# Second layer: third pair's projection and square moved ahead of pair 0's scores, and a new order of powers, masks, gathers and folds on GpSimd

## The chip, the cores and the metric

The kernel runs on one core of one Trainium2 chip. The metric is the device time of one execution in microseconds (us), lower is better. A core has a matrix engine (TensorE, PE in the rows), VectorE (DVE), ScalarE (ACT), GpSimd (POOL) and SyncE (SP), each with its own instruction queue that runs in order; they wait for each other through semaphores. What this kernel can tell from no change is about 0.2%, some 2.5 us.

## The reference

Two transformer-like layers over 8 batch items of 512 tokens with 128 features. In each layer an attention and a feed-forward branch work on the same normalised input, and both are added to it. Layer 1 has a banded 16-head attention and a top-1 mixture of eight experts. Layer 2, which the change touches, is this (the reference, cut):

```python
# layer 2, attention: 16 query heads of 64, one shared key/value head
xn = layernorm(x, g1)
q = xn @ Wq.T ; kv = xn @ Wkv.T            # k, v = 64 features each
q, k = l2norm(q) * 4, l2norm(k) * 4        # each head's vector divided by its length
sim = einsum('bhid,bjd->bhij', q, k)       # causal mask
out = einsum('bhij,bjd->bhid', softmax(sim), v)
attn = layernorm(out.reshape(b, n, 1024) @ Wout.T, g2)
# layer 2, feed-forward: weights are integers times 1/127
ffn = (silu(x @ wg.T) * (x @ wu.T)) @ wd.T
x = x + attn + ffn
```

## The kernel before, in words

Layer 1's attention takes the first part of the program, its experts the next, and layer 2 the last: from 619 us of the span on. Layer 2 runs once per batch item, seven times in a hardware loop and a last time (item 8) written out without the preparation of a next item. One trip is about 77 us.

The 16 heads go in 8 pairs (NP = 8), and `attend` on each engine has a loop `for n in range(NP)`, round n for pair n. Every engine's order of work is written out by hand, and a ring per PSUM bank or group of banks (Q, O, L, S, M, W, Z; `fillable`, `filled`, `emptied`) gives the semaphore values to wait for. In one round:

- TensorE: `scores(n)` (keys by queries, in three thirds), `project_q(n + 2)`, which makes the queries of the pair after next, `turn_q(n + 1)` (a transpose), for the first rounds a third of the feed-forward (`gate_up`), then `values1(n - 1)`. `sums1(0)` comes in round 5 and `sums1(1)` in round 6: they add up the exponentials of pairs 0 and 1, and of 2 and 3, for the softmax's denominators.
- ScalarE: three `exp_of(n, third)`, `squares(n + 2)` of the projected queries, `q_turned(n + 1)`, `gate_up(n + 1)`.
- VectorE: `q_sums` adds up the squares, `q_low(n + 1)`, `values_out(n - 1)`, then `q_unit(n + 2)`: it takes the length from GpSimd (L1958, L1960: scale and reciprocal) and multiplies the projected queries (L2011). That frees the projection's only PSUM bank (ring Q has one), so `project_q(n + 3)` can't start before it.
- GpSimd: `q_length` (L1272: the square root of the sums, as a power), then the causal masks of pair n (L1313, four selects in three groups, each group behind the exponentials of its third). Between them it prepares the next item: `fetch_slots` and `fetch` gather the experts' rows (L1231, two in round 1 and two in round 2), `both_roots` in round 4. And `fold(n)` (L1293) for pairs 0 to 3: a DMA from GpSimd's queue that adds block 1 of a pair's exponentials to block 0, so that `sums1` has less to read. In before `fold(n - 2)` is the first thing of rounds 2 to 5.

The name `arena` in rows is one big SBUF buffer, `late` its continuation for two pairs' exponentials, `ring_d` the projection's bank, `q_len`, `q_sum`, `q_rn` the lengths, their squares and reciprocals, `q_nat_sb` and `o_n` the two buffers of normalised queries.

Of the kernel before, what the change touches and what calls it, by code (L numbers as in the profile page):

```python
# [100 lines left out]
             sums=6, lens=6, q_lo=8, h1=3, masked=24, pv=4, added4=6, g_free=2, inverted=1, fin=1, stored=16,  # L101
             folded=16 * N_FOLD)

# [150 lines left out]
def two_layers(nc, x, wq, bq, wk, bk, wv, bv, wo, bo, w_router, w1, b1, w2, b2,  # L254
# [4 lines left out]
    with ExitStack() as ctx:  # L259
# [232 lines left out]
        def _(pe):  # L492
# [296 lines left out]
            def attend(b, last):  # L789
# [80 lines left out]
                def sums1(m):  # L870
# [3 lines left out]
                    if m < N_FOLD // 2:  # L874
                        pe.wait_ge(s["folded"].sem, s["folded"].at(b, 32 * (m + 1)))
                    if m == 2:
# [9 lines left out]
                pe.wait_ge(SR["r_free"].sem, SR["R"].emptied(b, "k.T"))  # L886
                gate_up(0)
                pe.wait_ge(SR["r_free"].sem, SR["R"].emptied(b, "q.T"))
                for n in range(NP):
                    scores(n)  # L890
                    if n + 2 < NP:
                        project_q(n + 2)
# [167 lines left out]
        def _(pool):  # L1060
# [219 lines left out]
            def attend(b, last):  # L1280
# [6 lines left out]
                def fold(n):  # L1287

                    pool.wait_ge(s["o_full"].sem, s["O"].filled(b, ("o", n)))
                    if n:  # L1290
                        pool.wait_ge(s["folded"].sem, s["folded"].at(b, 16 * n))
                    apart(pool)
                    pool.dma_start(probs_of(n, 0)[:, :, P:T], probs_of(n, 1),  # L1293
                                   accum_op=ALU.add).then_inc(s["folded"].sem, s["folded"].add(16))

                s["folded"].restart()
                for n in range(NP):
                    if 0 <= n - 2 < N_FOLD:
                        fold(n - 2)
                    if n + 2 < NP:  # L1300
# [15 lines left out]
                    if not last and n == 0:  # L1316
                        fetch_slots(b + 1)
                    if not last and n in (1, 2):
                        fetch(b + 1, (2 * n - 2, 2 * n - 1))
                    if not last and n == 4:  # L1320
# [17 lines left out]
        def _(act):  # L1338
# [156 lines left out]
            def attend(b, last):  # L1495
# [40 lines left out]

                gate_up(0)
                for n in range(NP):
                    for third in (0, 1, 2):
                        exp_of(n, third)  # L1540
                    if n + 2 < NP:
                        squares(n + 2)
                    if n + 1 < NP:
                        q_turned(n + 1)
                    if n + 1 < HC:
                        gate_up(n + 1)
# [658 lines left out]
```

## Time and profile before

| what | value |
|---|---|
| median of 3 runs | 1240.59 us (1240.56 to 1241.66) |
| the profiled execution's own time | 1239.02 us |
| its span, first to last instruction | 1237.2 us |
| TensorE busy, share of the span | 93% |
| VectorE, ScalarE, GpSimd busy | 74%, 54%, 40% |
| granted TensorE clock, mean | 0.98 |
| one trip of layer 2's loop | 77.0 us |

TensorE's busy share is an average over both layers. In one trip of layer 2 it is busy 72.8 of 77.0 us, and the rest is a handful of waits that return in each trip at the same place. A timeline's row gives a run of like instructions: start, length, engine, line, what it writes and reads, how many, and in brackets the idle time of the engine before it with the engine and line that ended it.

### The profile page before, as it was taken

The page shows a single profiled execution, that of the slowest core. Times are in us where ns is not written, and L with a number is a line of the kernel's source. Part 1 is how long each engine was busy: PE and PEld are TensorE (multiplying, and loading weights), DVE is VectorE, ACT ScalarE, POOL GpSimd, SP SyncE. Part 2 cuts the span into 40 slices and gives each one's busy share as a digit, 9 for nine tenths or more (in the row PEclk, how much of TensorE's full clock was granted, in tenths as well). Part 3 has the DMA queues.
Part 4 walks back from the last instruction along what each step waited for, and adds up shares of the span by engine and source line. Part 5 has one row for each costly group of instructions (what it writes and reads, how often), then busy time and mean ns, then how long its engine had stood idle before and what let it go on. Part 6 is the DMA issues. An engine that isn't in the chain of part 4 may idle for free.

```text
span 1237.2 us, 26393 instructions
## 1 busy us (share of the span) xinstructions
PE 1145.6 (93%) x8475; PEld 782.4 (63%) x8475; DVE 921.7 (74%) x2473; ACT 672.3 (54%) x1290; POOL 490.6 (40%) x691
## 2 busy tenths in 40 slices
PE   5999999999999998899399999999999999999996
PEld 3656666666666554799265857657576575765764
DVE  7888888888888897455456868668686686866755
ACT  2767676666676755355173552735527355273550
POOL 5122212121222311554364481744817448274450
PEclk8999999999999998899799999999999999999999
DMA  3311212020101000122011030210302103021020
GB/s 89 101 44 48 56 28 57 26 60 26 33 18 27 18 18 1 44 64 55 15 35 27 9 59 0 42 25 8 59 0 42 25 8 59 0 49 19 15 46 10
DMA packets 43718, 42.31 MB, mean 34 GB/s; under 512 B 7040, under 2 KB 36224, under 8 KB 43648
## 3 DMA queue, kind: packets, MB, share of 16 engines
q0 software_dynamic: 11008, 17.31, 8.0%
q1 hardware_dynamic: 32640, 24.15, 7.3%
q8 instruction: 34, 0.56, 0.2%
q14 instruction: 36, 0.29, 0.1%
HBM read 13.72 MB, written 6.75 MB: 17 GB/s over the span
## 4 chain that ended last, share of the span: by engine, by line
issue 19%; PE 11%; POOL 9%; DVE 7%; DMA 3%; ACT 1%; POOLq 0%; DVEq 0%; ACTq 0%
PE pair L496 4%; POOL q_len L1272 3%; DMA arena<-arena 3%; PE gather L496 2%; PE ring_d L496 2%; POOL arena L1231 2%; POOL arena L1313 2%; PE ring_a L496 1%; PE pair L500 1%; DVE q_len L1958 1%; DVE stats L1574 1%; POOL arena L1293 1%; DVE arena L2106 1%; DVE q_rn L1960 1%; ACT arena L1515 1%
## 5 line engine op out<-in xcount | busy, mean ns | idle before, releaser
L1378 ACT ACTIVATE arena<-ring_a 128x384 f32<-128x384 f32 (+1 forms) x512 | 253.6, 550 | 147.1 <-PE ring_a L496 146.9
L1126 POOL TENSOR_SCALAR_AFFINE_SELECT arena<-arena 128x512 f32<-128x512 f32 x128 | 82.4, 643 | 366.6 <-ACT arena L1378 366.4
L496 PE MATMUL ring_a<-q_max,rows 128*128 128x384 f32 (+1 forms) x512 | 197.2, 388 | 2.2 <-DVE q_max L1684 1.8
L1670 DVE CUSTOM_DVE_ANT_0 arena<-pair,arena 128x384 bf16<-128x384 f32 (+1 forms) x269 | 161.3, 614 | 23.6 <-PE pair L496 19.1
L1272 POOL TENSOR_TENSOR q_len<-q_sum,exponents 128x8 f32<-128x8 f32 x64 | 113.6, 1775 | 85.1 <-DVE q_sum L2000 85.1
L1535 ACT ACTIVATE arena<-ring_a 128x1024 f32<-128x1024 f32 x96 | 99.1, 1032 | 75.9 <-PE ring_a L496 75.7
L496 PE MATMUL ring_a<-q_parts,k_rows 64*128 64x384 f32 (+2 forms) x1152 | 128.3, 344 | 3.4 <-ACT q_parts L1523 2.4
L496 PE MATMUL ring_a<-arena,v_aug 128*32 128x384 f32 (+1 forms) x1024 | 123.5, 553 | 1.7 <-POOL arena L1126 0.6
L496 PE MATMUL pair<-arena,v_aug 128*64 128x512 f32 (+3 forms) x768 | 114.0, 439 | 3.4 <-ACT arena L1535 3.0
L496 PE MATMUL pair<-rows,q_rows 128*128 128x384 f32 (+1 forms) x269 | 110.0, 411 | 3.3 <-DMA rows<-k_rows 2.5
L496 PEld LDWEIGHTS ring_a<-q_max,rows 128*128 128x128 f32 x512 | 96.8, 191 | 21.4 <-ACT arena L1378 5.3
L496 PEld LDWEIGHTS ring_a<-q_parts,k_rows 64*128 64x128 f32 x1152 | 90.0, 187 | 23.7 <-issue 12.6
L1313 POOL TENSOR_SCALAR_AFFINE_SELECT arena<-arena 128x256 f32<-128x256 f32 x192 | 80.9, 531 | 45.5 <-ACT arena L1535 43.9
L496 PEld LDWEIGHTS pair<-arena,v_aug 128*64 128x64 f32 x768 | 51.1, 136 | 71.9 <-issue 58.7
L1670 DVE CUSTOM_DVE_ANT_0 arena<-gather,arena 128x512 bf16<-128x512 f32 (+1 forms) x124 | 78.2, 630 | 17.6 <-PE gather L496 11.4
L496 PEld LDWEIGHTS pair<-rows,q_rows 128*128 128x128 f32 x269 | 51.2, 191 | 57.4 <-DVE mx L1670 34.9
L2056 DVE COPY arena<-pair 128x512 f32<-128x512 f32 x64 | 44.2, 691 | 52.3 <-PE pair L496 51.8
L1670 DVE CUSTOM_DVE_ANT_0 arena<-ring_d,arena 128x384 bf16<-128x384 f32 (+1 forms) x119 | 73.2, 615 | 9.8 <-PE ring_d L496 6.5
L2000 DVE TENSOR_REDUCE q_sum<-arena 128x8 f32<-128x512 f32 x64 | 43.8, 684 | 44.6 <-ACT arena L1507 44.6
L496 PE MATMUL ring_d<-wq_sb,o_raw 128*128 128x128 f32 x384 | 55.6, 288 | 18.0 <-DVE o_n L2011 9.9
L496 PEld LDWEIGHTS ring_d<-wq_sb,o_raw 128*128 128x128 f32 x384 | 46.5, 191 | 37.5 <-DVE q_nat_sb L2011 18.3
L1440 ACT ACTIVATE arena<-ring_a,arena 128x128 f32<-128x128 f32 x156 | 43.6, 377 | 47.3 <-PE ring_a L496 46.9
(275 smaller groups left out, 2380.9 us busy)
## 6 DMA issues: line engine op xcount, KB each, us to landing
arena<-arena POOLq DMA_DIRECT2D x32, 384.0 KB, 4.6
rows<-k_rows SPq DMA_DIRECT2D x128, 64.0 KB, 2.0
arena<-in_w SPq DMA_DIRECT2D x16, 256.0 KB, 2.8
slots_y<-arena SPq DMA_DIRECT2D x39, 64.0 KB
x_all<-in_x SPq DMA_DIRECT2D x8, 256.0 KB, 3.8
tokens_x<-xn SPq DMA_DIRECT2D x8, 256.0 KB, 2.7
out<-o_t SPq DMA_DIRECT2D x8, 256.0 KB, 2.3
arena<-tokens_x,tokens_now POOLq DMA_INDIRECT x40
```

The lines of the kernel that those rows point to most:

```text
L496: return pe.matmul(out, lhs, rhs, start=start, stop=stop, skip_group_check=True)
L500: return [pe.transpose(slot[:, i * P:(i + 1) * P], tile_of(i), ident[:]) for i in range(n)][-1]
L1126: pool.affine_select(out=v, in_=v, compare_op=ALU.is_ge, fill=0.0, base=0, pattern=[[0, HG], [1 if late else -1, P]], channel_multiplier=- ...
L1231: pool.indirect_dma_start(y_back[:, i, :], None, slots_y[0:(TT + NE - 1) * P], bass.IndirectOffsetOnAxis(ap=slots_now[:, i:i + 1], axis=0) ...
L1272: pool.tensor_tensor(q_len[:, half], q_sum[:, half], exponents[:, 2 * NT:4 * NT], ALU.pow).then_inc(s["lens"].sem, s["lens"].add(1))
L1313: ins = pool.affine_select(out=v, in_=v, compare_op=ALU.is_ge, fill=0.0, base=0, pattern=[[0, 2], [1, P]], channel_multiplier=-1)
L1378: act.activation(probs[:, t % NT, h, 0:many], A.slot(("cols", c))[:, 0:many], ACT.Exp).then_inc(A.free.sem, A.free.add(1))
L1440: ins = act.activation(hidden[:, u % 2, c], hidden_bank(u, c), ACT.Relu, bias=staged[:, u, AT_B1 + c:AT_B1 + c + 1])
L1535: act.activation(dst, src, ACT.Exp).then_inc(ring.free.sem, ring.free.add(1))
L1670: dve.tensor_tensor_reduce(dump[:, h % 2, 0:many], M.slot(("max", n))[:, 0:many], masks[:, m, at:at + many], 1.0, LOWEST, ALU.add, ALU.max ...
L2000: dve.reduce_sum(q_sum[:, half_of(s, k)], q_sq, AX.X).then_inc(s["sums"].sem, s["sums"].add(1))
L2056: dve.tensor_copy(o1[:, n, :], ring.slot(("o", n))[:]).then_inc(ring.free.sem, ring.free.add(1))
```

## The change

Three things move; no arithmetic is added or taken away.

1. TensorE's `project_q(2)` and ScalarE's `squares(2)` stood in round 0 behind pair 0's scores and exponentials. They now stand behind `gate_up(0)`, ahead of round 0.
2. In each round GpSimd does the power first, then the masks, then gathers, then folds. Folds 0 and 1 come at the end of rounds 2 and 3, folds 2 and 3 at the end of round 4; before, one stood at the head of each of rounds 2 to 5. The gathers are one, two, one in rounds 0, 1, 2 and no longer two, two in rounds 1 and 2.
3. A fold no longer waits until the fold before it has landed: folds 0 and 1 count on one semaphore, 2 and 3 on another, and `sums1(0)` and `sums1(1)` wait for 32 on theirs.

```diff
-             folded=16 * N_FOLD)
+             folded0=32, folded1=32)
...
                     if m < N_FOLD // 2:
-                        pe.wait_ge(s["folded"].sem, s["folded"].at(b, 32 * (m + 1)))
+                        pe.wait_ge(s[f"folded{m}"].sem, s[f"folded{m}"].at(b, 32))
...
                 gate_up(0)
+                project_q(2)
                 pe.wait_ge(SR["r_free"].sem, SR["R"].emptied(b, "q.T"))
                 for n in range(NP):
                     scores(n)
-                    if n + 2 < NP:
+                    if 0 < n < NP - 2:
                         project_q(n + 2)
...
                 def fold(n):
                     pool.wait_ge(s["o_full"].sem, s["O"].filled(b, ("o", n)))
-                    if n:
-                        pool.wait_ge(s["folded"].sem, s["folded"].at(b, 16 * n))
+                    folded = s[f"folded{n // 2}"]
...
                 for n in range(NP):
-                    if 0 <= n - 2 < N_FOLD:
-                        fold(n - 2)
                     if n + 2 < NP:
                         q_length(s, n + 1, b)
...
                     if not last and n == 0:
                         fetch_slots(b + 1)
-                    if not last and n in (1, 2):
-                        fetch(b + 1, (2 * n - 2, 2 * n - 1))
+                    if not last and n < 3:
+                        fetch(b + 1, ((0,), (1, 2), (3,))[n])
+                    for of in {2: (0,), 3: (1,), 4: (2, 3)}.get(n, ()):
+                        fold(of)
...
                 gate_up(0)
+                squares(2)
                 for n in range(NP):
                     for third in (0, 1, 2):
                         exp_of(n, third)
-                    if n + 2 < NP:
+                    if 0 < n < NP - 2:
                         squares(n + 2)
```

TensorE's queue at the head of a trip, before and after (L798 and L802 are waits of the projection and of `gate_up`, L840 to L852 those of the scores):

```order
 L802 ISA
 L496 MATMUL ring_a<-q_rows,w_gu 128x512 x4
-L888 REGISTER_ALU
+L798 ISA
+L496 MATMUL ring_d<-wq_sb,o_raw 128x128 x4
+L889 REGISTER_ALU
 L840 REGISTER_ALU
 L841 ISA
```

The projection of pair 2 (ring_d) now stands between the feed-forward's first third and the wait ahead of pair 0's scores.

GpSimd's queue before, from the masks of round 2 to the power of round 3 (DMA arena<-slots_y is a gather, DMA arena<-arena a fold, TENSOR_TENSOR q_len the power):

```order
L1313 AFFINE_SELECT arena<-arena 128x2x128
L1231 DMA arena<-slots_y,slots_now 128x128 x2
L1289 REGISTER_ALU
L1291 ISA
L1293 DMA arena<-arena 128x2x384
L1270 REGISTER_ALU
L1272 TENSOR_TENSOR q_len<-q_sum,exponents 128x8
```

Two gathers, the wait for the last fold (L1291) and fold 1 stand ahead of the power. The same place of the changed kernel, whose lines have moved by one:

```order
L1312 AFFINE_SELECT arena<-arena 128x2x128
L1232 DMA arena<-slots_y,slots_now 128x128
L1290 ISA
L1293 DMA arena<-arena 128x2x384
L1271 REGISTER_ALU
L1273 TENSOR_TENSOR q_len<-q_sum,exponents 128x8
```

One gather and fold 0 stand there now. And the end of round 4 of the changed kernel, up to the power of round 5:

```order
L1312 AFFINE_SELECT late<-late 128x2x128
L1290 REGISTER_ALU
L1293 DMA arena<-arena 128x2x384
L1290 REGISTER_ALU
L1293 DMA arena<-arena 128x2x384
L1099 TENSOR_SCALAR veps<-mv 128x4
L1100 TENSOR_SCALAR veps<-mv 128x4
L1101 ISA
L1102 TENSOR_TENSOR rstd<-veps,exponents 128x8
L1271 REGISTER_ALU
L1273 TENSOR_TENSOR q_len<-q_sum,exponents 128x8
```

Folds 2 and 3 have moved ahead of `both_roots` (veps, rstd); before, fold 2 stood ahead of round 4's power and fold 3 between `both_roots` and round 5's power.

## Rows read from the trace of the kernel before

**Rows 1.** The page: busy time of each engine, and the projections' group.
```profile
PE 1145.6 (93%) x8475; PEld 782.4 (63%) x8475; DVE 921.7 (74%) x2473; ACT 672.3 (54%) x1290; POOL 490.6 (40%) x691
...
L496 PE MATMUL ring_d<-wq_sb,o_raw 128*128 128x128 f32 x384 | 55.6, 288 | 18.0 <-DVE o_n L2011 9.9
```

**Rows 2.** Busy time in windows, the third trip: length, then each engine's busy time.
```profile
773.90:850.90 77.00, 72.77 (x632) 51.36 (x632) 56.19 (x115) 38.35 (x60) 40.50 (x55) 1.00 0.15 27
```

**Rows 3.** Chain that ended last, third trip: start, length, what.
```profile
799.00 2.31 POOL q_len L1272
...
812.76 4.43 DMA arena<-arena
```

**Rows 4.** Timeline of TensorE: third trip, then seventh, then item 8.
```profile
773.91 1.11 PE L496 MATMUL ring_a<-q_parts,k_rows 64*128 64x384 f32 x12 [0.16 <-DVEq L2032]
...
776.34 1.16 PE L496 MATMUL ring_d<-wq_sb,o_raw 128*128 128x128 f32 x8
...
779.24 1.23 PE L496 MATMUL ring_a<-q_parts,k_rows 64*128 64x384 f32 x12 [0.28 <-ACT q_parts L1523]
...
782.15 1.16 PE L496 MATMUL ring_d<-wq_sb,o_raw 128*128 128x128 f32 x8 [0.54 <-DVE q_nat_sb L2011]
...
795.40 1.16 PE L496 MATMUL ring_d<-wq_sb,o_raw 128*128 128x128 f32 x8 [0.34 <-DVE q_nat_sb L2011]
...
802.92 1.16 PE L496 MATMUL ring_d<-wq_sb,o_raw 128*128 128x128 f32 x8 [1.50 <-DVE o_n L2011]
...
817.23 1.72 PE L496 MATMUL gather<-arena,pick_sum 128*32 128x512 f32 x24 [0.50 <-DMA arena<-arena]
...
1103.93 1.16 PE L496 MATMUL ring_d<-wq_sb,o_raw 128*128 128x128 f32 x8 [1.08 <-DVE q_nat_sb L2011]
...
1110.84 1.16 PE L496 MATMUL ring_d<-wq_sb,o_raw 128*128 128x128 f32 x8 [0.89 <-DVE o_n L2011]
...
1179.87 1.16 PE L496 MATMUL ring_d<-wq_sb,o_raw 128*128 128x128 f32 x8
```

**Rows 5.** Timeline of GpSimd, third trip.
```profile
795.53 1.39 POOL L1231 DMA_INDIRECT arena<-slots_y,slots_now  x1 [0.18 <-issue]
...
798.16 1.42 POOL L1293 DMA_DIRECT2D arena<-arena  x1
799.00 2.29 POOL L1272 TENSOR_TENSOR q_len<-q_sum,exponents 128x8 f32<-128x8 f32 x1
...
803.41 1.25 POOL L1293 DMA_DIRECT2D arena<-arena  x1 [0.65 <-DMA arena<-arena]
...
807.17 1.49 POOL L1313 TENSOR_SCALAR_AFFINE_SELECT late<-late 128x256 f32<-128x256 f32 x4
810.53 0.24 POOL L1098 TENSOR_SCALAR veps<-mv 128x4 f32<-128x4 f32 x1 [1.88 <-DVE mv L1583]
...
813.60 2.12 POOL L1272 TENSOR_TENSOR q_len<-q_sum,exponents 128x8 f32<-128x8 f32 x1
```

**Rows 6.** Timeline of VectorE, third trip, and one row of the seventh.
```profile
797.23 0.69 DVE L2000 TENSOR_REDUCE q_sum<-arena 128x8 f32<-128x512 f32 x1 [0.55 <-ACT arena L1507]
...
799.35 0.69 DVE L2056 COPY arena<-pair 128x512 f32<-128x512 f32 x1 [0.43 <-PE pair L496]
801.33 0.49 DVE L1958 TENSOR_SCALAR q_len<-q_len 128x8 f32<-128x8 f32 x1 [1.28 <-POOL q_len L1272]
...
1101.39 1.44 DVE L1958 TENSOR_SCALAR q_len<-q_len 128x8 f32<-128x8 f32 x1
```

**Rows 7.** Timeline of ScalarE, rounds 0 and 1 of the third trip.
```profile
775.27 1.03 ACT L1535 ACTIVATE arena<-ring_a 128x1024 f32<-128x1024 f32 x1
...
777.61 0.60 ACT L1507 ACTIVATE arena<-ring_d 128x512 f32<-128x512 f32 x1
...
783.35 0.60 ACT L1507 ACTIVATE arena<-ring_d 128x512 f32<-128x512 f32 x1 [0.41 <-PE ring_d L496]
```

**Rows 8.** The folds' line: who waited for it (us, times).
```profile
  PE gather L496: 4.0, 7
```

More of the change, by code:

```diff
@@ L1289, in fold @@
                     pool.wait_ge(s["o_full"].sem, s["O"].filled(b, ("o", n)))
-                    if n:
-                        pool.wait_ge(s["folded"].sem, s["folded"].at(b, 16 * n))
+                    folded = s[f"folded{n // 2}"]
                     apart(pool)
                     pool.dma_start(probs_of(n, 0)[:, :, P:T], probs_of(n, 1),
-                                   accum_op=ALU.add).then_inc(s["folded"].sem, s["folded"].add(16))
-                s["folded"].restart()
+                                   accum_op=ALU.add).then_inc(folded.sem, folded.add(16))
+                for name in ("folded0", "folded1"):
+                    s[name].restart()
                 for n in range(NP):
-                    if 0 <= n - 2 < N_FOLD:
-                        fold(n - 2)
                     if n + 2 < NP:
```

## The prediction, made before the changed kernel ran

> **What bounds the kernel now.** I read the page first: TensorE is busy 93% of the span and no other engine is near [rows 1]. That is an average over two layers, so I cut layer 2 into trips with the view by windows: a trip is 77.0 us with TensorE busy 72.77 [rows 2], so at most 4.2 us of a trip can be won by a new order. Next the timeline of TensorE, for the idle times in brackets [rows 4]. In the third trip they are 0.16 us ahead of pair 0's scores, 0.28 ahead of pair 1's, 0.54 ahead of pair 3's projection, 0.34 ahead of pair 5's, 1.50 ahead of pair 6's and 0.50 ahead of the second sums. The 1.50 returns in each of the first six trips, and the seventh has 1.08 and 0.89 in place of 0.34 and 1.50; the page's group agrees, 9.9 us of waits for the buffer o_n being 6 x 1.50 + 0.89 [rows 1]. Item 8 has no wait at these places: there GpSimd has no gathers, and pair 5's projection follows its predecessor at once [rows 4]. Then the chain of waits, to see what the two largest hang on: GpSimd's power in round 3, and a fold's DMA ahead of the second sums [rows 3].
>
> **The change part by part.**
>
> *GpSimd's power in round 3.* Its input, the sum of squares, starts at 797.23 and is there at 797.92 [rows 6]. But GpSimd is still at its second gather, then issues fold 1 from 798.16 for 1.42 us, to 799.58, and only then is the power worked off: it ends at 799.00 + 2.29 = 801.29, so it takes 1.71 from the end of the fold [rows 5]. VectorE, idle 1.28, starts on the length at 801.33 [rows 6], and TensorE starts pair 6's projection at 802.92, 1.59 later, having been ready at 802.92 - 1.50 = 801.42 [rows 4].
> In the changed order round 2 ends with one gather and fold 0. The gather starts at 795.53 as before and takes 1.39 [rows 5]; the fold follows at about 797.0 and takes 1.42, so GpSimd is free at about 798.5, some 0.6 after the sum is there. The power ends at 798.5 + 1.7 = 800.2. VectorE's copy of pair 2's values ends at 799.35 + 0.69 = 800.04 [rows 6], so it is not in the way, and the projection starts at 800.2 + 1.6 = 801.8 where TensorE is ready at 801.42. About 0.37 of the 1.50 stays: 1.13 us gained per trip, 6.8 over six trips. The bounds are 0 (the copy, a mask or the gather takes the place of the fold) and 1.50.
> In the seventh trip the waits are 1.08 and 0.89 [rows 4]. The second is of the same kind; I take 0.4 of it. Of the first, where VectorE's step on the length took 1.44 us in place of 0.49 [rows 6], I take half, 0.5. Together 0.9, between 0 and 2.0.
>
> *The folds and the second sums.* Fold 3 is issued at 812.76 and has landed 4.43 later [rows 3], and the sums start at 817.23 after 0.50 idle [rows 4]. Over seven trips this wait is 4.0 us [rows 8]. In the new order folds 2 and 3 follow the masks of round 4, which end at 807.17 + 1.49 = 808.66 now and 1.13 earlier then, at 807.5. Two issues of 1.25 [rows 5] end at 810.0. Fold 2 lands at about 807.5 + 4.4 = 811.9; fold 3 at 813.2 if the two don't hinder each other, and at 816.3 if its 4.43 only begins when fold 2 is in. TensorE gets there at 816.73 - 1.13 = 815.6. So the wait goes, 4.0 us gained, with 0 to 0.7 per trip coming back in the worst case. The wait of a fold for the fold before it, 0.65 in round 4 [rows 5], goes too, but at a place where GpSimd has time: round 4's power is not late for TensorE.
> What is late next: ahead of round 5's power now stand both folds and the roots. The roots take from 810.53 to 812.76, when the fold behind them starts [rows 3, 5]. After the change they can start when the second fold is issued, 810.0, end at 812.3, and the power starts there. Today it gets going when fold 3's issue is done, 812.76 + 1.25 = 814.0, which is 812.9 in the shifted time. It keeps 0.6 us of slack; VectorE's normalisations and block sums, which hang on it, move with it.
>
> *Powers first, in the other rounds.* In round 2 nothing stands in the power's way today when the sum is there: fold 0 is issued before it. So the 0.34 ahead of pair 5's projection stays: 0 gained, between 0 and 0.34. The gather moved to round 0 falls into time in which GpSimd waits; 0, with a bound of 0.1 either way.
>
> *The projection and the square moved ahead.* TensorE does the same work. The projection (1.16 long, the next matmul starting some 1.0 after its start) fills the 0.16 wait and pushes pair 0's scores from 773.91 to about 774.75 [rows 4]. ScalarE decides here: from 775.27 it goes through exponentials, square (777.61), turned queries and gate without a gap, until it waits 0.41 at 783.35 for pair 3's projection [rows 7]. With the square first (from 775.27, when the projection is there) it has 0.5 us of its own work done earlier, but the first exponential starts about 0.6 later, since it must wait for the later scores; the exponentials free the bank for the gate's second third, so that third is 0.4 to 0.6 later, and with it pair 1's scores (0.2 to 0.3 later), whose last third waits for the gate to be copied out. Followed through, pair 3's projection is ready to start at about 782.1, against 782.15 now. The 0.54 wait there and the 0.28 ahead of pair 1's scores are not saved but turned into waits for ScalarE. I take 0. The bounds per trip are a gain of 0.98, if all three early waits (0.16 + 0.28 + 0.54) go, and a loss of 0.4, if VectorE's length step, now at 780.0 beside the masks of round 0, is held up by them. Eight items make -7.8 to +3.2 us of it; the middle of my walk is the value.
>
> *The sum.* 6.8 + 0.9 + 4.0 + 0 + 0 = 11.7 us less than the profiled execution's 1239.02 (a span of 1237.2 and 1.8 around it): 1227.3. That execution was 1.57 below the median 1240.59, so against the median the forecast is 1228.9 us, 0.94% faster.
>
> **The rivals.**
>
> *VectorE is held off by the masks.* The step on the length (L1958) is an operation on 128x8 numbers that took 1.44 us once, at 1101.39 beside four masks, and 0.49 at 801.33 beside the same kind [rows 6]. After the change VectorE reaches it in round 3 when the masks have just begun. If it loses by 0.95 more each trip, 1.13 shrinks to 0.18: 7 x 0.95 = 6.6 us less gain, 1235.5 us; with the same in round 0, at 0.4 for eight items, 1238.7. Against it: in the rows the masks let it in after one or two of them in all but one case.
> The Trainium skill (SBUF — State Buffer, section Who interferes with whom) says that GpSimd and some VectorE operations, tensor_scalar among them, share one port pair under an exclusive lock, and that whoever is first keeps it for the whole instruction while the other is fully blocked. By that rule the step would wait for one mask at most; the 1.44 us at 1101.39 is longer than the rule gives, so the trace agrees with a lock and not with its length.
>
> *The second folds clog GpSimd's queue: slower.* Nothing in the trace shows two folds issued back to back. If the second issue can't start until the first is in (4.4 us), fold 3 is issued at 807.5 + 4.4 = 811.9 to 813.2, the roots run to 815.4 and the power of round 5 to 817.1, where today its end at 813.60 + 2.12 = 815.72 [rows 5] would be 814.6 in the shifted time. Pair 7's low part on VectorE, behind the normalisation and the block sums, then comes about 2.5 us late for the scores: 1.7 gained per trip, 2.5 lost, 7 x 0.8 = 5.6 us slower, 1246 us. It decides once the hold is over about 3.6 us: with 4.4 a trip loses 0.8, and each us of hold is one of loss. Against it: today fold 1 is issued right behind two gathers, in 1.42 us, with no hold [rows 5].
>
> *Given back later.* From round 5 on VectorE does block sums and normalisations without much rest. If it set the pace of rounds 6 and 7, TensorE would arrive earlier and wait there: about 1239 to 1240, no change. Against it: VectorE itself waits for round 5's power, and that power moves forward by as much.
>
> *More goes than I count.* If the 0.34 of six trips (2.0) and a third of the early waits (2.6) go too: about 1224.
>
> **How the numbers follow.** Forecast as worked out, 1226 to 1232: 0.52. VectorE held off, 1232 to 1238: 0.20. More than counted, 1221 to 1226: 0.13. Given back, within 0.2% (about 2.5 us, what a measurement here tells from no change): 0.07. Clogged queue, or any other loss: 0.08. The predicted time is 1228.9. The range that leaves out about 2 in 10 goes from 1224.5 to 1237.5. Faster by over 0.2%: 0.85; within: 0.07; slower: 0.08.
>
> **What would show it.** In the changed kernel's timeline the wait ahead of pair 6's projection should be 0.3 to 0.5 us in the first six trips, the one ahead of the second sums gone, the 0.34 ahead of pair 5's projection still there, the trip 75.4 us long, and pair 3's projection as far behind the gate's first third as now, with new short waits for ScalarE ahead of it. VectorE's step on the length in round 3 shows the first rival by its duration: about 0.5 for me, 1.4 for it. Two folds issued 1.3 us apart refute the second. The prediction is wrong if the wait of round 4 stays above 1 us, if the early part of the trip gains or loses more than 0.4 us, or if a new wait of over 0.5 us shows up in rounds 5 to 7.

## The result: 1233.6 us, and the profile after

| | median, us | lowest to highest |
|---|---|---|
| before, 6 runs | 1241.12 | 1240.45 to 1245.00 |
| changed kernel, 6 runs | 1233.64 | 1229.94 to 1237.76 |

The ratio is 0.9933, with a 95% interval from 0.991 to 0.9956: faster, about 7.5 us. Forecast were 1228.9 us and a range from 1224.5 to 1237.5. The direction is right and the time lies in the range; the gain is about two thirds of the 11.7 us summed up.

The six runs of the changed kernel differ by 7.8 us among themselves, those of before by 4.6. Layer 1 and the experts, which the change does not touch, have a share in such differences: layer 2 begins at 616.4 us of the span in the profiled execution before (its first matmul; ScalarE's first copy is at 619) and at 619.5 after, and over the thirteen profiles of this study anywhere from 607.1 to 620.5. So I compare layer 2 alone, and in it the trips, from one copy of the gate's first third on ScalarE to the next:

| | trips 1 to 7, us | item 8 and the end | layer 2 |
|---|---|---|---|
| before | 78.31, 76.99, 77.01, 77.01, 77.08, 76.69, 77.01 | 80.7 | 620.8 |
| after | 77.12, 75.74, 75.72, 75.70, 75.70, 75.68, 75.56 | 82.3 | 613.5 |

The third column is what is left of layer 2: item 8 to the end of the span, and 2.2 us ahead of the first copy. The trips gain 8.9 us, and item 8 with the end loses 1.6. The view by windows, of the third trip after (columns as in [rows 2]): us, busy time of PE, PEld, DVE, ACT and POOL with instructions, granted clock, DMA.

```profile
775.00:850.70 75.70, 72.51 (x634) 51.28 (x634) 56.07 (x115) 38.32 (x60) 41.86 (x56) 1.00 0.15 28
```

TensorE's busy time is 72.51 here and was 72.77 [rows 2]: the trip became shorter by its waits. The timeline of TensorE in this trip shows which, beside [rows 4]:

```profile
773.23 1.20 PE L496 MATMUL ring_a<-q_rows,w_gu 128*128 128x512 f32 x4 [0.26 <-DVE k_rows L2027]
774.27 1.05 PE L496 MATMUL ring_d<-wq_sb,o_raw 128*128 128x128 f32 x8
775.25 1.08 PE L496 MATMUL ring_a<-q_parts,k_rows 64*128 64x384 f32 x12
778.02 0.66 PE L500 MATMUL pair<-ident,o_n 128*128 128x128 f32 x4 [0.59 <-ACT arena L1536]
778.94 1.20 PE L496 MATMUL ring_a<-q_rows,w_gu 128*128 128x512 f32 x4 [0.26 <-ACT arena L1536]
781.75 0.97 PE L496 MATMUL ring_a<-q_parts,k_rows 64*128 64x512 f32 x6 [0.19 <-ACT arena L1516]
782.65 1.16 PE L496 MATMUL ring_d<-wq_sb,o_raw 128*128 128x128 f32 x8
795.99 1.16 PE L496 MATMUL ring_d<-wq_sb,o_raw 128*128 128x128 f32 x8 [0.33 <-DVE q_nat_sb L2013]
802.89 1.16 PE L496 MATMUL ring_d<-wq_sb,o_raw 128*128 128x128 f32 x8 [0.89 <-DVE o_n L2013]
816.64 1.72 PE L496 MATMUL gather<-arena,pick_sum 128*32 128x512 f32 x24
823.86 2.38 PE L496 MATMUL pair<-arena,v_aug 128*64 128x512 f32 x16 [0.41 <-ACT arena L1536]
```

The first row is the gate's first third, the second the moved projection. The three early waits were 0.16, 0.28 and 0.54 [rows 4]; now they are 0.59, 0.26 and 0.19, all for ScalarE. Pair 3's projection (782.65) has no wait of its own any more; it starts 9.42 us after the gate's first third, before 9.58 (from 772.57 to 782.15). Ahead of pair 5's stands 0.33 (before 0.34), ahead of pair 6's 0.89 (before 1.50), and the second sums (816.64) start at once (before 0.50). GpSimd and VectorE in rounds 2 to 5, beside [rows 5] and [rows 6]:

```profile
796.11 1.32 POOL L1232 DMA_INDIRECT arena<-slots_y,slots_now  x1 [0.18 <-issue]
797.44 1.39 POOL L1293 DMA_DIRECT2D arena<-arena  x1
798.59 2.43 POOL L1273 TENSOR_TENSOR q_len<-q_sum,exponents 128x8 f32<-128x8 f32 x1
800.23 2.23 POOL L1312 TENSOR_SCALAR_AFFINE_SELECT arena<-arena 128x256 f32<-128x256 f32 x4
808.59 2.41 POOL L1293 DMA_DIRECT2D arena<-arena  x2
811.66 1.67 POOL L1102 TENSOR_TENSOR rstd<-veps,exponents 128x8 f32<-128x8 f32 x1
813.31 1.63 POOL L1273 TENSOR_TENSOR q_len<-q_sum,exponents 128x8 f32<-128x8 f32 x1
```

```profile
797.82 0.69 DVE L2002 TENSOR_REDUCE q_sum<-arena 128x8 f32<-128x512 f32 x1 [0.56 <-ACT arena L1508]
798.82 0.69 DVE L2021 TENSOR_TENSOR q_parts<-arena,q_parts 128x512 fp32r<-128x512 f32 x1 [0.32 <-ACT q_parts L1524]
801.05 0.73 DVE L1960 TENSOR_SCALAR q_len<-q_len 128x8 f32<-128x8 f32 x1 [0.42 <-POOL q_len L1273]
```

The fold ends at 797.44 + 1.39 = 798.83, and the sum at 798.51, so the fold holds the power up by 0.3 us, where the working had 0.6. But the power ends at 798.59 + 2.43 = 801.02, which is 3.58 after the fold began; before it was 3.13 (798.16 to 801.29 [rows 5]). And VectorE's step on the length takes 0.73 where it took 0.49. The two folds of round 4 are issued in 2.41 us together, and round 5's power begins at 813.31.

**Where item 8 loses.** The page of either kernel has a wait of 1.90 us near the end, where TensorE waits for the last normalisation. What follows differs. After, in windows from that wait on:

```profile
1211.80:1213.80 2.00, 0.10 (x2) 0.08 (x1) 1.93 (x4) 0.00 (x0) 0.00 (x0) 1.00 0.00 0
1213.80:1216.00 2.20, 1.94 (x7) 1.35 (x8) 2.12 (x4) 0.00 (x0) 0.00 (x0) 0.79 0.00 0
1216.00:1218.00 2.00, 2.00 (x10) 1.90 (x10) 0.60 (x2) 0.00 (x0) 0.00 (x0) 0.50 0.00 0
1218.00:1220.00 2.00, 2.00 (x17) 1.96 (x16) 1.00 (x2) 0.00 (x0) 0.00 (x0) 0.88 0.00 0
```

Before, the same stretch:

```profile
1217.60:1219.60 2.00, 0.10 (x2) 0.11 (x1) 1.93 (x4) 0.00 (x0) 0.00 (x0) 1.00 0.00 0
1219.60:1221.80 2.20, 1.94 (x12) 1.35 (x12) 2.12 (x4) 0.00 (x0) 0.00 (x0) 1.00 0.00 0
1221.80:1223.80 2.00, 2.00 (x18) 1.92 (x18) 1.28 (x3) 0.00 (x0) 0.00 (x0) 1.00 0.00 0
```

The third column from the end is the granted clock. Behind the same 1.90 us of idle TensorE it stays at 1.00 (2.4 GHz) before, and falls to 0.50 (1.2 GHz) after. From the end of the idle time to the end of the span it is 17.7 us before and 19.3 after: 1.6 us. Up to the end of that wait item 8 takes the same in both. Which of the other kernels show it stands behind the experiments.

### The profile page after: what moved, and what is told of

Read it like the earlier page. It is cut to its first block, busy times and chain, and to the rows that moved or that the text cites. A ratio compares the mean times of both kernels' runs of the same rounds, so it can differ in the third digit from the quotient of the medians.

```text
span 1233.0 us, 26372 instructions
## 1 busy us (share of the span) xinstructions
PE 1148.4 (93%) x8475; PEld 785.9 (64%) x8475; DVE 920.7 (75%) x2473; ACT 671.5 (54%) x1290; POOL 495.5 (40%) x691
## 4 chain that ended last, share of the span: by engine, by line
issue 17%; PE 17%; POOL 10%; DVE 5%; ACT 1%; POOLq 0%; DVEq 0%; ACTq 0%
PE pair L496 7%; PE gather L496 4%; PE ring_a L496 3%; POOL arena L1312 3%; POOL arena L1232 3%; POOL q_len L1273 3%; PE ring_d L496 2%; PE pair L500 1%; DVE q_len L1960 1%; POOL arena L1293 1%; DVE arena L2108 1%; ACT arena L1536 1%; DVE q_rn L1962 0%; DVE q_nat_sb L2013 0%; DVE o_n L2013 0%
## 5 line engine op out<-in xcount | busy, mean ns | idle before, releaser
L1127 POOL TENSOR_SCALAR_AFFINE_SELECT arena<-arena 128x512 f32<-128x512 f32 x128 | 82.4, 643 | 366.8 <-ACT arena L1379 366.6
L1273 POOL TENSOR_TENSOR q_len<-q_sum,exponents 128x8 f32<-128x8 f32 x64 | 111.0, 1735 | 87.1 <-DVE q_sum L2002 87.1
L1312 POOL TENSOR_SCALAR_AFFINE_SELECT arena<-arena 128x256 f32<-128x256 f32 x192 | 83.7, 545 | 42.3 <-ACT arena L1536 41.4
L496 PEld LDWEIGHTS gather<-wout_sb,arena 128*128 128x128 f32 x512 | 66.7, 195 | 2.5 <-DVE arena L2108 0.6
L496 PE MATMUL gather<-wout_sb,arena 128*128 128x128 f32 x512 | 67.5, 279 | 0.3 <-DVE arena L2108 0.3
```

The costliest lines, as they stand in the source:

```text
L496: return pe.matmul(out, lhs, rhs, start=start, stop=stop, skip_group_check=True)
L1127: pool.affine_select(out=v, in_=v, compare_op=ALU.is_ge, fill=0.0, base=0, pattern=[[0, HG], [1 if late else -1, P]], channel_multiplier=- ...
L1273: pool.tensor_tensor(q_len[:, half], q_sum[:, half], exponents[:, 2 * NT:4 * NT], ALU.pow).then_inc(s["lens"].sem, s["lens"].add(1))
L1312: ins = pool.affine_select(out=v, in_=v, compare_op=ALU.is_ge, fill=0.0, base=0, pattern=[[0, 2], [1, P]], channel_multiplier=-1)
```

## The experiments

They ran in three groups, each with runs of before beside it: the first four experiments (before there: 1231.01 us, 14 runs) on chip 4, the next four (1242.00, 19 runs) and the last three (1242.84, 7 runs) on chip 0. Ratios are to the runs of before in the same group. "Trip" is the third trip unless several are given, the waits are those of TensorE in it.

**1. The projection and the square alone, on the kernel before.**

```diff
                 gate_up(0)
+                project_q(2)
...
-                    if n + 2 < NP:
+                    if 0 < n < NP - 2:
                         project_q(n + 2)
```

(and the same for ScalarE's squares.)

> The kernel before with only the projection of pair 2 and its square moved ahead of pair 0's scores; GpSimd as before. A trip of layer 2's loop takes 77.01 us before and 75.70 us after. If the two parts of the change add up, this one is worth the 0.16 us by which pair 3's projection stands nearer to the trip's start (9.58 us before, 9.42 us after): trips of 76.85 us, the waits of round 4 (1.50 us) and of the second sums (0.50 us) unchanged, 1.2 us in all, no measurable change. The rival, that the early square also helps the powers of later rounds, gives 76.3 us or less and a wait of round 4 below 1.2 us.

Measured: ratio 1.0001 (0.9982 to 1.0021), trip 76.97 against 77.01. The early waits are 0.58, 0.26 and 0.17 as in the changed kernel, but ahead of pair 5's projection stand now 1.04 instead of 0.34, and ahead of pair 6's 0.88 instead of 1.50. VectorE's rows say why:

```profile
786.59 1.40 DVE L1960 TENSOR_SCALAR q_len<-q_len 128x8 f32<-128x8 f32 x1
794.15 0.73 DVE L1960 TENSOR_SCALAR q_len<-q_len 128x8 f32<-128x8 f32 x1 [0.42 <-POOL q_len L1273]
```

In round 2 the step meets the masks and takes 1.40 us. The move alone makes no difference that can be measured, and it shifts the other engines against each other.

**2. GpSimd's order and the folds' semaphores alone, on the kernel before.** The edit is the change without the lines of experiment 1.

> The changed kernel with the projection and the square back in their old place; only GpSimd's order and the folds' two semaphores are new. If the parts add up: a wait of round 4 of 0.89 us, none ahead of the second sums, the three early waits (0.16, 0.28, 0.54 us) as before, trips of 77.01 - 0.61 - 0.50 = 75.9 us, and about 7 us less than before. If the early part is needed for GpSimd to be in time, the wait of round 4 stays above 1.2 us and trips at 76.2 us or more.

Measured: ratio 0.9899 (0.9865 to 0.9933), trips 75.54 to 75.61 from the third to the fifth. No wait ahead of pair 5's projection, 1.01 ahead of pair 6's, none ahead of the second sums. Here the power ends in good time, and the step takes back what was won:

```profile
786.51 1.39 POOL L1292 DMA_DIRECT2D arena<-arena  x1
787.88 1.73 POOL L1272 TENSOR_TENSOR q_len<-q_sum,exponents 128x8 f32<-128x8 f32 x1
789.51 1.52 POOL L1311 TENSOR_SCALAR_AFFINE_SELECT arena<-arena 128x256 f32<-128x256 f32 x4
```

```profile
789.70 1.37 DVE L1958 TENSOR_SCALAR q_len<-q_len 128x8 f32<-128x8 f32 x1
```

The power ends 3.10 after the fold began, the step takes 1.37 beside all four masks. So GpSimd's order with the folds' semaphores is the whole gain (which part of it the semaphores are worth, experiment 8 asks), and the wait ahead of pair 6's projection stays near 1 us whichever of the two causes feeds it.

**3. VectorE's low part reads one SBUF operand in place of two.** The low part is the difference of the turned queries and their rounded copy, both in SBUF. Here it is a PSUM bank times zero minus the rounded copy, so it is not the real low part, and the exact scores are left out.

> The changed kernel, but VectorE's low part of the turned queries (rounds 0 to 5 of each item) is computed from a PSUM bank times zero minus the high part, so this operation reads one operand from SBUF and no longer two; the low part is then wrong and the exact scores are left out. In the changed kernel the power of round 3 is dispatched behind fold 0 and ends at 801.02 us, 3.58 us after the fold's start, where before it was 3.13; VectorE's low part runs from 798.82 to 799.51, just when the fold's 1.39 us are over (798.83). Theory A, the power is held off while an operation with two SBUF operands has the shared way into SBUF: the power ends 0.4 to 0.5 us earlier against the fold's start (3.1 us), the wait ahead of pair 6's projection falls from 0.89 to about 0.45 us, trips of 75.25 us, about 3 us less in all. Theory B, the fold's issue itself lasts longer behind one gather than behind two: the 3.58 us, the wait of 0.89 and trips of 75.7 us stay.

Measured: ratio 0.9926 (0.9898 to 0.9954), trip 75.47. The power ends 3.10 after the fold's start, no longer 3.58, but the step takes 1.43 and the wait is 1.08. The power moved as expected; the wait did not follow, so the run is a miss for the forecast wait. Nor does it show why the power moved: the low part also starts at another moment, 1.52 us after the fold's start and no longer 1.38.

**4. No step on the length.** The reciprocal takes the length directly, its factor is in the next multiplication; the bound of the length from below is left out.

```diff
-                dve.tensor_scalar(length, length, scale, NORM_EPS, ALU.mult, ALU.max).then_inc(s["own"].sem, s["own"].add(1))
-                dve.wait_ge(s["own"].sem, s["own"].at(b, s["own"].n))
+                if scale == 1.0:
+                    dve.tensor_scalar(length, length, scale, NORM_EPS, ALU.mult, ALU.max).then_inc(s["own"].sem, s["own"].add(1))
+                    dve.wait_ge(s["own"].sem, s["own"].at(b, s["own"].n))
```

> The changed kernel without VectorE's step on the queries' lengths (scale by 16 and the lower bound of 1e-12): the reciprocal takes the length as it is and the factor 16 goes into the next multiplication, so only the lower bound is left out. The step takes 0.73 us in round 3, 0.38 in round 2 and 0.49 in round 4 of the changed kernel beside GpSimd's masks, 0.16 where GpSimd rests. Theory A, that step alone is held off by the masks, since the reciprocal behind it always takes 0.20 us: the wait ahead of pair 6's projection falls from 0.89 by 0.73 + 0.04 to about 0.12 us, the one ahead of pair 5's (0.33) goes, trips of 74.6 us, 8 us less than the changed kernel in all. Theory B, whatever VectorE starts beside the masks is held off: the reciprocal takes 0.7 us in round 3, the wait falls by 0.2 us at most, trips of 75.4 us or more.

Measured: ratio 0.9845 (0.9812 to 0.9877), trip 73.89. No wait is left ahead of pair 5's or pair 6's projection. So without an instruction on 128x8 numbers a trip is 1.8 us shorter than the changed kernel's; the two waits are 1.22 of that (0.33 and 0.89), an idle time of 0.15 ahead of pair 7's projection goes too, the wait for the keys ahead of the gate falling from 0.26 to 0.16 is another 0.1, and the rest is not at one place. This is not the price of the step alone: here the power, too, ends 3.10 us after the fold's start and not 3.58.

**5. Fold 0 behind the power of round 3, too.**

```diff
-                    for of in {2: (0,), 3: (1,), 4: (2, 3)}.get(n, ()):
+                    for of in {3: (0, 1), 4: (2, 3)}.get(n, ()):
```

> The changed kernel with fold 0 moved from the end of round 2 to round 3, behind its power. Theory (round 3's power ends late because it stands behind a fold and meets VectorE's low part): the power is worked off as soon as the sum is there, some 0.3 us earlier than a fold in front lets it, and the wait ahead of pair 6's projection falls from 0.89 to 0.4 us where the step on the length takes 0.4 to 0.7; trips of about 75.2. Rival (only the step on the length against the masks decides): the step takes up to 1.4, the wait stays at 0.9 to 1.1, trips at 75.5 or more.

Measured: ratio 0.9858 (0.9834 to 0.9882), trip 74.93. The power starts when the sum is there and the projection (796.96) follows the scores without a wait:

```profile
790.93 1.32 POOL L1232 DMA_INDIRECT arena<-slots_y,slots_now  x1 [0.17 <-issue]
793.41 1.66 POOL L1273 TENSOR_TENSOR q_len<-q_sum,exponents 128x8 f32<-128x8 f32 x1 [1.16 <-DVE q_sum L2002]
796.50 2.56 POOL L1293 DMA_DIRECT2D arena<-arena  x2
```

```profile
796.96 1.16 PE L496 MATMUL ring_d<-wq_sb,o_raw 128*128 128x128 f32 x8
```

Of the 0.89 us 0.75 go, more than the 0.5 expected; an idle time of 0.14 is left, too short for the timeline to print it (the scores end at 796.83). The step takes 0.49: an earlier power meets the masks at another moment. The rival, that only the step decides, falls. Of the kernels here that leave nothing out this one has the shortest trips and the lowest ratio: 0.77 us a trip less than the changed kernel. The interval of its ratio lies wholly below that of the changed kernel (from 0.991), but overlaps those of experiments 2 and 9.

**6. GpSimd's masks wait for the step.** One wait ahead of the masks of rounds 0 to 5:

```diff
                         q_length(s, n + 1, b)
+                        pool.wait_ge(s["own"].sem, s["own"].at(b, (1, 4, 7, 10, 12, 14)[n]))
```

> The changed kernel in which GpSimd starts the masks of rounds 0 to 5 only when VectorE has done its step on the length. Theory (the step is held off by the masks, and that is what is left of the waits ahead of pairs 5 and 6): the step takes 0.16 to 0.2 us in every round, the wait ahead of pair 6's projection falls from 0.89 to about 0.3, the short one ahead of pair 5's goes, trips of 74.2 to 74.9. Rival (the masks then come late for the values that are multiplied by them): new waits behind them, trips of 75.7 or more.

Measured: ratio 1.0013 (0.9997 to 1.0029), trip 76.26, its neighbours 77.66 and 77.31. The step takes 0.17 in every round, as expected, and the wait ahead of pair 6's projection is 0.92 all the same:

```profile
799.13 1.94 POOL L1313 TENSOR_SCALAR_AFFINE_SELECT arena<-arena 128x256 f32<-128x256 f32 x4 [0.45 <-DVE q_rn L1963]
801.24 1.27 POOL L1232 DMA_INDIRECT arena<-slots_y,slots_now  x1 [0.17 <-issue]
802.52 1.39 POOL L1293 DMA_DIRECT2D arena<-arena  x1
803.37 2.25 POOL L1273 TENSOR_TENSOR q_len<-q_sum,exponents 128x8 f32<-128x8 f32 x1
```

The power before these masks ended at 798.68, and they start 0.45 later; then they take 1.94, not 1.48, as VectorE's next instructions run beside them. Gather, fold and power follow that much later. The time that VectorE saved GpSimd lost, and GpSimd's stream is what the power stands in. Ahead of pair 5's projection stands more than before, 0.68 in this trip and in the seventh and 1.42 to 1.46 in the others, where the changed kernel has 0.33. In the fourth trip, one of the others, the masks of rounds 1 and 2 take 2.48 us each time. Neither theory had this: the step went as mine said, the trip as the rival's.

**7. The same wait on the kernel of experiment 2.**

> GpSimd's new order alone (projection and square where they stood before), with the same wait of the masks. Theory: as in the run above without the low part's meeting with the power, so the waits ahead of pairs 5 and 6 are 0.3 us or less, trips 74.0 to 74.5, from 75.5 without the wait. Rival: no better than 75.5.

Measured: ratio 1.0013 (0.9994 to 1.0032), trip 76.77, with 0.70 and 1.06 of waits ahead of pairs 5 and 6 (1.44 or 1.45 ahead of pair 5's in all other trips). A miss, for the same reason.

**8. Each fold waits until the one before it has landed**, at the new places.

```diff
                     pool.wait_ge(s["o_full"].sem, s["O"].filled(b, ("o", n)))
+                    if n:
+                        before_it = s[f"folded{(n - 1) // 2}"]
+                        pool.wait_ge(before_it.sem, before_it.at(b, 32 if n == 2 else 16))
```

> The changed kernel with each fold waiting until the one before it has landed, as in the kernel before, at the new places. If the two folds of round 4 may only pass because each has a semaphore of its own: fold 3 is issued 4.4 us or more after fold 2, the roots and round 5's power come 2 to 3 us later, trips are 76.5 to 77.5 or longer. Rival (GpSimd has the time to spare there): trips within 0.2 of 75.7.

Measured: ratio 1.0096 (1.0064 to 1.0128), trip 78.37.

```profile
814.37 1.18 POOL L1296 DMA_DIRECT2D arena<-arena  x1
819.33 1.19 POOL L1296 DMA_DIRECT2D arena<-arena  x1 [3.77 <-issue]
821.18 1.68 POOL L1102 TENSOR_TENSOR rstd<-veps,exponents 128x8 f32<-128x8 f32 x1
822.84 1.64 POOL L1273 TENSOR_TENSOR q_len<-q_sum,exponents 128x8 f32<-128x8 f32 x1
```

```profile
823.78 1.72 PE L496 MATMUL gather<-arena,pick_sum 128*32 128x512 f32 x24 [1.51 <-DMA arena<-arena]
```

Fold 3 is issued 4.96 us after fold 2, and the sums wait 1.51. The new places work only because the folds have no order among themselves any more: at these places that part is worth 2.7 us of a trip, twice what the whole change gained.

**9. Experiments 2 and 5 together**: GpSimd's order with fold 0 behind the power, projection and square where they stood.

> The kernel before with GpSimd's new order alone and fold 0 behind round 3's power (projection and square where they stood before). Theory (no fold in front of the power, and the move of the projection costs 0.1 to 0.2 us a trip): the early waits are 0.16, 0.28 and 0.54 again, none over 0.3 ahead of pair 6's projection, trips of 74.7 to 74.9. Rival (the two do not add up, as the step on the length meets the masks otherwise): trips of 75.3 or more.

Measured: ratio 0.9872 (0.9837 to 0.9908), trip 75.11; the waits are 0.16, 0.30, 0.54 and 0.32, none ahead of pair 6's projection. Between my 74.9 and the rival's 75.3, but longer than the trip of experiment 5, not shorter: with the fold out of the way the moved projection gains 0.18 us a trip (74.93 against 75.11).

**10. Experiments 4 and 5 together.** The bound of the length is left out as in 4.

> The run with fold 0 behind round 3's power, and the step on the length left out as in the earlier run (the bound of the length from below is left out of the computation). Theory (the fold's place matters only through the wait ahead of pair 6's projection, which is gone without the step): trips of 73.8 to 74.0, as with the fold in front. Rival (the fold's place is worth something of its own): 73.5 or less, or, where the later fold 0 holds something up, 74.3 or more.

Measured: ratio 0.9802 (0.9772 to 0.9832), trip 73.94 against 73.89 with the fold in front. As expected, the fold's place matters only through the wait ahead of pair 6's projection.

**11. Powers first and nothing else, on the kernel before.**

```diff
-                    if 0 <= n - 2 < N_FOLD:
-                        fold(n - 2)
                     if n + 2 < NP:
                         q_length(s, n + 1, b)
+                    if 0 <= n - 2 < N_FOLD:
+                        fold(n - 2)
```

> The kernel before with one edit: in each round the power stands ahead of the fold; the gathers, the folds' rounds and their one semaphore are as before. Theory: the wait ahead of pair 6's projection falls from 1.50 to 0.5 us or less, but fold 3 now stands behind the roots and round 5's power, is issued at least 1.6 us later, and the wait ahead of the second sums grows from 0.50 to 3 us or more: trips of 78 to 79. Rival (folds have time to spare, and powers first is all of the gain): trips of 75.5 to 76.

Measured: ratio 1.0291 (1.0259 to 1.0324), trips 80.49 to 83.02. Worse than expected, in two places that I had not seen. The fold now stands ahead of the masks in round 2, the masks run beside it and take 2.44 us, and the two gathers and the power follow late:

```profile
813.34 1.71 POOL L1272 TENSOR_TENSOR q_len<-q_sum,exponents 128x8 f32<-128x8 f32 x1
```

```profile
817.04 2.08 PE L496 MATMUL ring_d<-wq_sb,o_raw 128*128 128x128 f32 x8 [2.05 <-DVE o_n L2011]
834.31 1.72 PE L496 MATMUL gather<-arena,pick_sum 128*32 128x512 f32 x24 [2.11 <-DMA arena<-arena]
```

So the wait ahead of pair 6's projection did not fall but rose to 2.05, of which the step on the length, 0.85 in place of 0.49, is a part, and the sums wait 2.11. And behind the first of these the projection takes 2.08 us, not 1.16. The windows show the granted clock:

```profile
812.00:815.00 3.00, 2.99 (x34) 2.13 (x30) 1.18 (x2) 1.07 (x2) 2.87 (x3) 1.00 0.16 44
817.00:819.00 2.00, 1.96 (x9) 1.96 (x10) 1.78 (x2) 0.00 (x0) 1.34 (x3) 0.50 1.14 186
819.00:820.00 1.00, 1.00 (x7) 0.67 (x7) 0.22 (x1) 0.60 (x1) 0.00 (x0) 0.50 0.10 12
820.00:824.00 4.00, 4.00 (x38) 2.62 (x40) 2.52 (x6) 1.61 (x3) 3.45 (x5) 0.97 0.01 1
```

TensorE had nothing to do for 2.05 us and then ran at 0.50, 1.2 GHz, for some 3 us. This trip is 3.48 us longer than before's; the two waits are 2.16 of that (0.55 and 1.61), and the slower clock is the likely source of most of the other 1.3. A wait of this length can cost more than its length, but not each does. This profile has thirteen idle times of 1.90 us or more in layer 2's items; the clock falls at or within 1 us of the end of ten of them, and not at the 2.11 and one 2.15 of the sums, nor at the 1.90 near the end. The trips with two falls (the second, fourth and sixth) take 82.4 to 83.0 us, the third, fifth and seventh with one 80.5 to 81.2. In experiment 8 an idle time of 2.62 us in the first trip is followed by no fall.

## Why the prediction was right in direction and off in size

By its own steps, the third trip for one of a kind:

| step | forecast | measured |
|---|---|---|
| GpSimd's power in round 3, per trip | 1.13 | 0.61 |
| wait ahead of the second sums, per trip | 0.50 gone | 0.50 gone |
| wait ahead of pair 5's projection | 0.34 stays | 0.33 |
| projection and square moved, third trip | 0 | 0.16 gained |
| second folds held up | no | no: two issued in 2.41 us |
| trip | 75.4 | 75.7 |
| item 8 and the end | no change | 1.6 lost |

*The power in round 3: the step that was mis-sized.* "About 0.37 of the 1.50 stays" is wrong: 0.89 stays. TensorE was ready at 802.89 - 0.89 = 802.00. The fold began 4.56 us ahead of that (797.44), by my working 4.42 (797.0 and 801.42): 0.14 better. But the power ended 3.58 after the fold's start where I had 3.2 (797.0 and 800.2): 0.38 worse. From the power's end to the projection it was 1.87 where I had 1.6: 0.27 worse, nearly all of it the step on the length, 0.73 in place of 0.49. Together 0.51, and 0.52 is what the wait came out above the forecast. I had considered one neighbour of the power, the copy of the values, and found it out of the way. The one that meets it is the low part (L2021), which reads two SBUF operands. In the kernels of this study in which a fold stands directly before the power:

| kernel | fold's issue, us | low part starts after the fold's start | power ends after the fold's start |
|---|---|---|---|
| before, round 3 | 1.42 | 0.07 | 3.13 |
| experiment 7 | 1.39 | 0.00 | 3.09 |
| experiment 6 | 1.39 | 0.29 | 3.10 |
| experiment 7, round 4 | 1.24 | 1.22 | 3.44 |
| experiment 8 | 1.39 | 1.37 | 3.57 |
| changed kernel | 1.39 | 1.38 | 3.58 |
| experiment 1, round 3 | 1.42 | 1.45 | 3.65 |
| experiment 4 | 1.39 | 1.54 | 3.09 |
| experiment 1, round 2 | 1.39 | 1.56 | 3.11 |
| experiment 2 | 1.39 | 1.57 | 3.10 |

(Of a kernel without a round it is the one where the fold stands before pair 6's power.) The low part takes 0.69 us. Where it is running when the fold's issue ends, or starts up to 0.03 us behind it, the power ends 1.5 us after the low part does (801.02 - 799.51 = 1.51 after, 806.80 - 805.29 in experiment 8, 794.12 - 792.61 in experiment 1). Where it is over by then, or starts 0.15 us or more behind it, the power takes no notice. With one SBUF operand less (experiment 3) it takes none either, 3.10, but its low part also began behind the harmful moment, as in experiments 2 and 4, so this run agrees and does not decide. No run moves the low part and nothing else: that it is the low part that holds the power up is read from this pattern, ten cases without an exception. The Trainium skill (SBUF — State Buffer, section Who interferes with whom) says that a VectorE instruction with two SBUF inputs contends with a GpSimd instruction that reads SBUF, and that the order of issue decides who blocks. By that rule the low part, if first, holds the power up; the table agrees, at 0.47 to 0.52 us (3.57 and 3.58 against 3.10, 3.65 against 3.13).

*The first rival, VectorE held off by the masks.* It had a chance of 0.20, and it is there, in smaller size: 0.73 in place of 0.49 in round 3, not 1.44. With another phase between the engines it comes in full: 1.40 in experiment 1, 1.37 in experiment 2, 1.43 in experiment 3, each time beside all four masks: the rule of the Trainium skill that I cited, by which it would wait for one mask at most, is not borne out. Without the step no wait is left ahead of pairs 5 and 6 (experiment 4), but with it and an earlier power only 0.14 is left ahead of pair 6 (experiment 5): the wait hangs on the chain of both, and of the 0.52 us too much in round 3 the step's share is 0.24 (0.73 against 0.49). I held against the rival that "the masks let it in after one or two of them in all but one case". That was a statement on one phase of the trip. The change shifts the phase, so the one odd case was the evidence to weigh.

*The second sums and the folds.* As worked out: fold 3 is issued before 811.0 and the sums start at 816.64 without a wait. The median from issue to landing is 4.8 us, 4.6 before, the longest 6.9, so two folds at once do slow each other a little, and there was room for it. The rival of a clogged queue is refuted by the 2.41 us for both, and experiment 8 shows what it would have cost.

*The early part.* My walk said that the waits turn into waits for ScalarE, and they did (0.59, 0.26, 0.19), at 0.16 to 0.21 us in favour in the second to the seventh trip (in the third 9.42 against 9.58). In the first trip, where before has no wait ahead of pair 0's scores, the way from the gate's first third to pair 3's projection is 0.37 longer (11.69 against 11.32), and in item 8 0.10 shorter (9.28 against 9.38), though its early waits are 0.99 together and were 0.72. Together that is 0.9 us gained. I had 0, between a gain of 0.98 and a loss of 0.4 per item. Experiments 5 and 9 show 0.18 a trip. Experiment 1 shows that it can be eaten at once: there the waits ahead of pairs 5 and 6 are 1.92 together, before they are 1.84.

*The seventh trip and the end.* I had 0.9 for the seventh trip's two waits: 1.08 and 0.89 are now 0.33 and 0.90, 0.74 gained. The end lost 1.6 us to the granted clock, behind a wait of 1.90 us that the change does not touch. All thirteen profiles have this wait. In the changed kernel's and in those of experiments 2, 3, 4, 6, 7 and 8 the clock falls behind it, in the one before and in those of experiments 1, 5, 9, 10 and 11 it doesn't. From the end of the wait to the end of the span it is 18.1 to 19.3 us in the seven profiles with the fall and 17.0 to 17.8 in the six without; experiments 4 and 10, which have the same code here, take 18.1 and 17.0. No run here shows what decides it, and whether it is so in each execution of a kernel stays open.

The sum by measured terms: 6 x 0.61 + 0.74 + 4.0 for the sums + 0.9 for the early part - 1.6 = 7.7 us, against 7.3 by which layer 2 is shorter and 11.7 forecast. Of the missing 4.0, 3.1 are the power's term, 0.2 the seventh trip's and 1.6 the clock's, with 0.9 back from the early part. So the largest term was sized wrong by nearly half, outside the 0.3 to 0.5 us of wait that I had named for it; the measured time lies in the range all the same.

*What stays open.* In experiment 6 the trips go up and down between 76.3 and 77.7 with the wait ahead of pair 5's projection (0.68 or 1.42 to 1.46), and why the masks take 1.94 in some and 2.48 in others I have not followed. No run tries the folds' separate semaphores alone, or the gathers' new rounds alone. In before and in the changed kernel ScalarE's square in round 2 begins some 0.5 us late, which it does not in experiments 1 to 4; it is off TensorE's path. And no run shows a place for the step at which the masks never meet it; experiments 6 and 7 say only that making GpSimd wait costs as much as it saves.

## What to carry to other kernels

When a wait hangs on a chain through two engines that share a resource, price each link by its worst row, not by its usual one: a change of order moves all phases, and a rare 1.4 us becomes the rule in the next version. Leave a short instruction that other engines can hold off out of the critical chain altogether, rather than protecting it with a wait, which costs the other engine what it saves. And where transfers wait for one another without a need, try a second semaphore before tuning their places.

## What the runs showed of the hardware

- A VectorE instruction on 128x8 numbers takes 0.16 to 0.17 us alone and 0.2 to 1.44 beside GpSimd's selects (masks) of 128x256. At 1.37 to 1.44 it ends with the fourth of them: it is held off through several instructions, not one. The other way round, four selects take 1.94 us, in other trips 2.48, beside VectorE's multiplications (experiment 6), and 1.48 in experiment 5.
- A GpSimd power that reads SBUF ended 0.47 to 0.52 us later (3.57 and 3.58 us against 3.10 after the issue before it began, 3.65 against 3.13) where VectorE's instruction with two SBUF operands was running as GpSimd's preceding issue ended (it began from 0.02 before to 0.03 us after that end), and not where it was over before or began 0.15 us after.
- Two accumulating transfers of 384 KB, one issued behind the other, take GpSimd 2.41 us together, and land after 4.8 us in the median.
- TensorE idle for 1.95 to 2.73 us was followed by about 3 us at a granted clock of 0.50 (1.2 GHz) ten times in one execution (experiment 11), while 2.11 and 2.15 there and 2.62 in experiment 8 were not; an idle time of 1.90 us was in seven of the thirteen profiles and not in six. Idle times of 1.5 us (before, six times) were not.
